# Grams moved beside the y products, state work moved one slot ahead, in a hybrid SSM and expert kernel

## The reference

```
lcs  = cumsum(dt * A)                       # decay sums inside the chunk
M    = exp(where(mask, lcs_l - lcs_i, -inf))
G    = C @ B^T                              # the gram of the chunk
y    = (M * G) @ x  +  exp(lcs) * C @ h     # own part + carried state
h    = exp(lcs_last) * h + (M_last * x)^T @ B
```

## Time and profile before

| | us |
|---|---|
| median of 3 runs | 580.51 (578.98 to 584.52) |
| profiled execution | 576.64 |
| its span, first to last instruction | 574.9 |
| PE busy in the span | 548.7 |
| DVE busy | 437.6 |
| ACT busy | 356.2 |
| POOL busy | 172.6 |

### The profile page before, as it was taken

The page is one execution under the profiler, slowest core; times in us unless marked ns, Lnnn a source line. Parts: engine busy times, 40 slices in busy tenths (PEclk is TensorE's granted clock), DMA queues, the critical chain, the costliest instruction groups (busy, mean ns, idle before and its releaser), DMA issues.

```text
span 574.9 us, 11864 instructions
## 1 busy us (share of the span) xinstructions
PE 548.7 (95%) x4016; PEld 429.8 (75%) x4016; DVE 437.6 (76%) x1037; ACT 356.2 (62%) x767; POOL 172.6 (30%) x232
## 2 busy tenths in 40 slices
PE   8886999999999999999999999999999999999996
PEld 7665767877777777877787777777778787777774
DVE  4878767887789785888688786987768787676654
ACT  3894488637675477636795477745787376852442
POOL 2073504521163202631046201622036210542011
PEclk9999999999999999999999999999999999999999
DMA  6650006300550006600272004700064003510120
GB/s 204 183 152 2 0 33 190 84 1 2 147 173 3 1 6 175 143 1 0 81 173 65 0 0 155 164 0 0 15 198 106 0 1 105 157 44 1 38 59 21
DMA packets 37354, 41.43 MB, mean 72 GB/s; under 512 B 3482, under 2 KB 27716, under 8 KB 37316
## 3 DMA queue, kind: packets, MB, share of 16 engines
q1 hardware_dynamic: 36724, 40.80, 25.9%
q10 hardware_dynamic: 592, 0.15, 0.1%
HBM read 37.79 MB, written 3.15 MB: 71 GB/s over the span
## 4 chain that ended last, share of the span: by engine, by line
PE 48%; DVE 19%; issue 11%; ACT 9%; DMA 5%; POOL 5%; SPq 1%; DVEq 0%; ACTq 0%; POOLq 0%
PE bank L424 7%; PE bank L426 5%; PE bank L425 5%; PE bank L535 4%; PE bank L642 4%; PE bank L644 4%; PE bank L643 4%; DVE act_l L1268 4%; DVE cv L1121 4%; DMA grow<-lc_rows 3%; ACT act_h L874 3%; PE bank L547 2%; PE bank L563 2%; PE bank L435 2%; ACT L967 2%
## 5 line engine op out<-in xcount | busy, mean ns | idle before, releaser
L1268 DVE SCALAR_TENSOR_TENSOR act_l<-bank,act_h 128x512 fp32r<-128x512 f32 x192 | 131.3, 686 | 69.8 <-ACT act_h L874 68.6
L874 ACT ACTIVATE act_h<-bank 128x512 fp32r<-128x512 f32 x192 | 114.1, 594 | 81.9 <-PE bank L426 78.0
L424 PE MATMUL bank<-fTl,w1h 128*128 128x512 f32 x192 | 86.9, 452 | 3.0 <-DVE fTl L1219 2.3
L1492 POOL TENSOR_TENSOR late<-late 128x512 f32<-128x512 f32 x31 | 39.8, 1285 | 163.3 <-DVE late L1276 163.3
L894 ACT ACTIVATE seg<-seg,lneg 128x128 f32<-128x128 f32 x256 | 81.2, 391 | 2.8 <-DMA seg<-lc_rows 2.8
L642 PE MATMUL bank<-act_l,w2h 128*128 128x512 f32 x192 | 77.5, 404 | 1.6 <-DVE act_l L1268 1.5
L425 PE MATMUL bank<-fTh,w1l 128*128 128x512 f32 x192 | 75.7, 394 | 0.0
L644 PE MATMUL bank<-act_h,w2h 128*128 128x512 f32 x192 | 75.6, 394 | 0.0
L426 PE MATMUL bank<-fTh,w1h 128*128 128x512 f32 x192 | 75.6, 394 | 0.0
L643 PE MATMUL bank<-act_h,w2l 128*128 128x512 f32 x192 | 75.2, 392 | 0.0
L1479 POOL TENSOR_TENSOR xw<-xs,seg 128x128 f32<-128x128 f32 x48 | 19.9, 414 | 157.3 <-ACT seg L894 82.8
(11 more groups left out here) (176 smaller groups left out, 1063.6 us busy)
## 6 DMA issues: line engine op xcount, KB each, us to landing
seg<-lc_rows SPq DMA_DIRECT2D x32, 512.0 KB, 4.5
late<-gk_rows SPq DMA_DIRECT2D x8, 1024.0 KB, 9.3
grow<-lc_rows SPq DMA_DIRECT2D x48, 128.0 KB, 5.4
x_in<-L_attn_hidden_dram SPq DMA_DIRECT2D x8, 256.0 KB, 3.7
out_dram<-late SPq DMA_DIRECT2D x8, 256.0 KB, 2.5
late<-L_ffn_sw_dram SPq DMA_DIRECT2D x2, 512.0 KB, 7.2
late<-L_ffn_rw_dram SPq DMA_DIRECT2D x1, 1024.0 KB, 7.7
CT<-L_attn_w_in_proj_dram SPq DMA_DIRECT2D x1, 512.0 KB, 5.3
```

The lines of the kernel that those rows point to most:

```text
L424: mm(dst, stat_h, mov_l, start=True, stop=False)
L874: nc.scalar.activation(act_h[:, b % RING, :], HID[b % 2][:], ACT.Relu).then_inc(act_h_ready, 1)
L1268: v_.scalar_tensor_tensor(act_l[:, r, :], HID[b % 2][:], 0.0, f(act_h[:, r, :]), ALU.max, ALU.subtract)\
```

## The change

1. Chunks 1 to 3 have their gram in front of the y product of the chunk before (inside `y_product`, step 2) and no longer in a step 1 of their own. Chunk 0's gram stays.
2. The chunk's own state product moves from step 2 to step 1 (`state_product`), and in sequences 1 to 7 DVE's state update moves with it (`next_state`, now in slots 13, 16 and 19, behind `act_l`).
3. DVE's `mg` of chunks 1 to 3 splits: the first half goes to slots 15, 18 and 21, the second to 16, 19 and 22, each **behind** the slot's `act_l`. In the opening it stays where it was.
4. `dta` and `kept` are stored with a stride of 32 columns per chunk, so that four 32-column matmuls become one of full width, in `lcs` and in `g_transposes`, where it becomes a transpose.
5. ACT copies B's fourth block ahead of the relu of slot 6, and moves `xs_copy(0)` from slot 5 to slot 6. DVE does only the first tap of the second convolution in slot 2, and the other three in slot 3.

```diff
 def lcs(s):
-    for c in range(NCH):
-        ins = mm(sums[32 * c:32 * c + 32, P:2 * P], dta[:, c * NH:c * NH + 32], upto[:], start=True, stop=True)
+    mm(sums[:, P:2 * P], dta[:].rearrange("p c q -> p (c q)"), upto[:], start=True, stop=True).then_inc(lcs_psum, 1)
...
+def state_product(s, c):
     if c > 0:
         pe.wait_ge(state_step, nth(s, 8, (2, 5, 8)[c - 1]))
+    pe.wait_ge(btok_ready, nth(s, 3, c + 1))
+    pe.wait_ge(xw_ready, nth(s, 6, 2 * c + 2))
+    for n in range(NP):
+        ins = mm(MAIN[1][:, n * 64:(n + 1) * 64], btok[:, at(n)], xw[:, n, :, :].rearrange("p t d -> p (t d)"),
+                 start=True, stop=True)
+    ins.then_inc(s_psum, 1)
+
+def y_product(s, c):
+    if c == NCH - 1:
+        pe.wait_ge(state_step, nth(s, 8, 8))
     if c < NCH - 1:
-        pe.wait_ge(btok_ready, nth(s, 3, c + 1))
-        pe.wait_ge(xw_ready, nth(s, 6, 2 * c + 2))
-        for n in range(NP):
-            ins = mm(MAIN[1][:, n * 64:(n + 1) * 64], btok[:, at(n)], xw[:, n, :, :].rearrange("p t d -> p (t d)"),
-                     start=True, stop=True)
-        ins.then_inc(s_psum, 1)
+        gram(s, c + 1, None)
...
-    if b == 0:
+    if b == 0 and c == NCH - 1:
         pe.wait_ge(mg_ready, nth(s, 8, 2 * c + 2))
...
 def g_transposes(s, prev):
-    for c in range(NCH):
-        ins = mm(MAIN[2][32 * c:32 * c + 32, 0:P], kept[:, c * NE:c * NE + 32], ident[:], start=True, stop=True)
-    ins.then_inc(gT_psum, 1)
+    nc.tensor.transpose(MAIN[2][:, 0:P], kept[:].rearrange("p c q -> p (c q)"), ident[:]).then_inc(gT_psum, 1)
...
 # PE, scan_part
-    if step == 1:
+    if step == 1 and c == 0:
         gram(s, c, prev)
+    if step == 1 and c < NCH - 1:
+        state_product(s, c)
...
 # ACT, body
+    if s is not None and i == 6:
+        b_copy(s, 3)
     if new := block_at(i, prev, older):
         relu(*new)
-    if s is not None and i in (5, 6):
-        b_copy(s, i - 3)
-        xs_copy(s, i - 5)
+    if s is not None and i == 5:
+        b_copy(s, 2)
+    if s is not None and i == 6:
+        xs_copy(s, 0)
+        xs_copy(s, 1)
...
 # DVE, body
     if (new := block_at(i, prev, older)) and not (i == 0 and prev is not None):
         act_low(*new)
+    if s is not None and i in (15, 18, 21):
+        masked_gram(s, i // 3 - 4, 0)
+    if s is not None and i in (16, 19, 22):
+        masked_gram(s, i // 3 - 4, 1)
+    if s is not None and i in (13, 16, 19):
+        next_state(s, i // 3 - 4)
...
-            conv(s, 1, (0, 1))
+            conv(s, 1, (0,))
         if i == 3:
-            conv(s, 1, (2, 3))
+            conv(s, 1, (1, 2, 3))
```

More of the change, by code:

```diff
@@ L180, in build @@
         rank = sb("rank", [P, NCH * NE])
-        kept = sb("kept", [P, (NCH - 1) * NE + 32])
+        kept = sb("kept", [P, NCH, 32])
         gT = sb("gT", [P, P])
@@ L704, in scan_part @@
                         b_tokens(s, c, prev, older)
-                    if step == 1:
+                    if step == 1 and c == 0:
                         gram(s, c, prev)
-                        if c == NCH - 1 and not is_seq(s, n_seq - 1):
-                            proj(s + 1, 0)
+                    if step == 1 and c < NCH - 1:
+                        state_product(s, c)
+                    if step == 1 and c == NCH - 1 and not is_seq(s, n_seq - 1):
+                        proj(s + 1, 0)
                     if step == 2:
@@ L785, in opening @@
                         b_tokens(0, c, None, None)
-                    gram(0, c, None)
+                    if c == 0:
+                        gram(0, c, None)
                     if c < 2:
@@ L1144, in c_copy @@
                 v_.tensor_copy(CT[:, b, :], MAIN[b][:]).then_inc(c_ready, 1)
-            def attend(s, c, step):
[L1147 to L1154, removed]
-                if step == 2:
[L1157 to L1173, removed]
@@ new lines, in masked_gram @@
+            def masked_gram(s, c, hf):
+                dve.wait_ge(g_psum, nth(s, 8, 2 * c + hf + 1))
+                dve.wait_ge(decay_masked, nth(s, 8, 2 * c + hf + 1))
+                if hf == 0 and (v := nth(s, 4, c)) is not None:
+                    dve.wait_ge(y_psum, v)
+                v_.tensor_tensor(mg[:, hf], MAIN[2 + hf][:].rearrange("p (n l) -> p n l", n=NP), decay(c)[:, hf], ALU.mult)\
+                    .then_inc(mg_ready, 1)
+            def attend(s, c, step):
+                if step == 1 and (c == 0 or is_seq(s, 0)):
+                    masked_gram(s, c, 0)
+                    masked_gram(s, c, 1)
+                if step == 2:
+                    if c < NCH - 1 and is_seq(s, 0):
+                        next_state(s, c)
@@ L1182, in attend, with next_state @@
                     v_.tensor_tensor(yT[:, :, at(c)], yT[:, :, at(c)], szT[:, :, at(c)], ALU.mult).then_inc(yz_ready, 1)
+            def next_state(s, c):
+                first = (0, 2, 5)[c]
+                if c > 0:
+                    dve.wait_ge(grow_ready, nth(s, 3, c))
+                    v_.tensor_tensor(state_m[:], state[:, (c - 1) % 2], grow[:, c % 2, :, P - 1:P].to_broadcast([P, NP, 2 * HD]),
+                                     ALU.mult).then_inc(state_step, 1)
+                    dve.wait_ge(state_step, nth(s, 8, first + 1))
+                    first += 1
+                dve.wait_ge(s_psum, nth(s, 3, c + 1))
+                own = MAIN[1][:, 0:256].rearrange("p (n d) -> p n d", n=NP)
+                for t in range(2):
+                    q, d = slice(64 * t, 64 * t + 64), slice(HD * t, HD * t + HD)
+                    if c == 0:
+                        v_.tensor_copy(state[q, c % 2, :, d], own[q, :, d]).then_inc(state_step, 1)
+                    else:
+                        v_.tensor_tensor(state[q, c % 2, :, d], own[q, :, d], state_m[q, :, d], ALU.add).then_inc(state_step, 1)
+                dve.wait_ge(state_step, nth(s, 8, first + 2))
             def mean_square(s):
@@ L1431, in opening @@
                                 channel_multiplier=1).then_inc(tables_set, 1)
-                for t, v in ((ones[:], 1.0), (upto[:], 1.0), (turn[:], 0.0), (lower[:], 1.0), (center[:], -1.0 / P), (dta[:, NCH * NH:], 0.0), (kept[:, NCH * NE:], 0.0)):
+                for t, v in ((ones[:], 1.0), (upto[:], 1.0), (turn[:], 0.0), (lower[:], 1.0), (center[:], -1.0 / P), (dta[:, :, NH:], 0.0), (kept[:, :, NE:], 0.0)):
                     g.memset(t, v).then_inc(zeros_set, 1)
```

12 lines of the change are left out of this document (6 added, 6 removed).

## The result

| | before | after |
|---|---|---|
| median, same chip, 4 runs each | 580.73 us | 607.31 us (606.22 to 613.5) |
| profiled execution | 576.64 us | 607.24 us |
| its span | 574.9 us | 605.5 us |
| mean distance from one `lcs` to the next, sequences 1 to 7 | 66.34 us | 70.38 us |

The ratio is **1.0497, interval 1.0448 to 1.0546**. On the median of 580.51 that is 609.4 us: slower, as forecast, but 8 us above the 601 predicted, and just beyond the range. It grew by 4.04 us, where +2.98 was forecast. Where a slot is said to grow, its length is taken from the first matmul of the first layer in the slot before to that in the slot itself.

The account below looks back on a forecast made before the run. TensorE, busy 548.7 of 574.9 us, was taken as the bound; 3.93 - 0.31 - 0.64 = +2.98 us for each of seven sequences, with opening and end +21.2, gave 601 us predicted, range 588 to 609.

Parts of the forecast that it names:

- the waits behind `act_l`: Slots 17, 20, 23: TensorE waits for the second `mg`, 2.42 us chain; 2 x 1.39 + 1.15 = 3.93 us per sequence lost.
- chunk blocks and state work: TensorE's gram, state and y product blocks: fewer tile-shape surcharges save 0.31 us per sequence, 0.61 as other bound.
- front part: Widened `lcs` and gate transpose, earlier copy of B: saves 0.64 us per sequence (0.2 to 1.3).
- the clock: Rival: each of 21 new waits drops TensorE's clock and loses some 1.6 us more; 635 us, chance 3%.
- Chunk 0 is spared: Chunk 0 adds no wait, as its `mg` stays ahead of `act_l`.
- worse: Rival: later `mg` of chunk 1 delays the decay reload two chunks on, up to 1 us more per sequence; 608, chance 6%.
- change of shape: Between state and y product on TensorE: its removal estimated at 0.07 us, three times per sequence (0.21).
- a full-width record: Widened TensorE matmuls: each full-width fp32 record costs about 0.116 us (0.93 / 8).
- The price of a gram in front of a y product: TensorE's joint blocks: kept at 1.09 us, the only price in the rows.

Follow-up runs that it names:

- e11: Kernel before with only the store's DMA moved behind the decay and growth reloads; 575.7 us against 578.09, ratio 0.9961.
- e7: e6 with the store's DMA moved behind the decay and growth reloads; 570.07 us, ratio 0.9884 against the kernel before.
- e8: Changed kernel with second `mg` ahead of `act_l`, store's DMA behind the reloads and `hn` moved from slot 18 to 19; 573.85 us, ratio 0.9936 against before.
- e5: Changed kernel with only the store's DMA moved behind the decay and growth reloads; 599.64 us against 577.56 for the kernel before, ratio 1.0400.
- e1: Changed kernel with DVE's second `mg` of chunks 1 to 3 ahead of `act_l` again; 586.7 us against 578.5 for the kernel before, ratio 1.0149.
- e2: Kernel before with only DVE's second `mg` of chunks 1 to 3 moved behind the slot's `act_l`; 597.6 us against 578.5, ratio 1.0323.
- e6: Kernel before with only the front part's edits (widened `lcs` and gate transpose, new ScalarE and convolution order); 580.23 us against 577.56, ratio 1.0024.
- e4: e1 with the state product and VectorE's state update back in step 2; 586.73 us, ratio 1.0136 against the kernel before.

## Why the prediction was right in kind and wrong in size

From before to after leads a path over four of the kernels (e11, e7, e8, e5), each read from one trace, so the period's +4.04 splits into their steps:

| step | from to | forecast | measured |
|---|---|---|---|
| the waits behind `act_l`, slots 17, 20, 23 | e8 to e5 | +3.93 | +3.64 |
| chunk blocks and state work | e7 to e8 | -0.31 | +0.04 |
| front part | e11 to e7 | -0.64 | -0.53 |
| store's chain, taken away from before | before to e11 | 0 | -0.29 |
| store's chain, put back into the change | e5 to after | 0 | +0.91 |
| the clock in sequence 1 | e5 to after | 0 | +0.27 |
| sum | before to after | +2.98 | +4.04 |

(`hn` leaves slot 18 from e7 to e8 and comes back from e8 to e5. With `mg` behind `act_l` it seems to make no wait of its own: slot 20 grows by 1.43 us (sequence 1 left out), and slot 17, with no `hn`, by 1.37. That is argued from the slots; no kernel had `hn` later and `mg` behind.)

**The added wait: right.** It is the largest term by far, its mechanism is in the rows (2.40 us where 2.42 was forecast), e1 takes it out of the changed kernel and e2 puts it into the kernel before. The slots, less what they grow in e8, give 1.37 + 1.43 + 1.04 = 3.84. What I missed is a refund: behind slot 23 TensorE is late, so the small wait for `act_l` in slot 0 ends by itself, -0.23.

**"Chunk 0 is spared": the step that failed.** True of the order of its `mg`, and I looked at nothing else. Chunk 0's `mg` also needs the decays, which hang on a reload, which stands behind a store in SyncE's queue, which waits for VectorE. That chain left 0.16 us of wait at the decays of sequence 4 before, and no room. What the front part brought TensorE to `lcs` sooner was paid back at the decays (e6), and the gram of chunk 1 in front of slot 14's y product made the rest. Net of what the chain cost before, that is 0.91 - 0.29 = 0.62 us of the period, and from `lcs` of sequence 2 to the end 7.7 us between e5 and the change, less 2.4 between e11 and before: some 5 us in all, the largest part of what was missing.

The sign stood in the trace of the kernel before. In its waits of TensorE, between the two lines shown in the earlier trace rows, there is a third:

```profile
PE bank L563 <- DVE mg L1153: 2.7, 5, 0.9
```

Three of these five are chunk 0's `mg`, in slot 14 of sequences 3, 6 and 7. One of them, 0.87 us long, is in the earlier trace rows, where I took from it only the 0.74 us from VectorE to TensorE, and did not ask why that `mg` was late.

Among the rivals, "worse" named late reloads, with up to 1 us per sequence, but of later chunks, through `mg` of chunk 1 freeing a buffer late. ScalarE's waits for DMAs tell the two apart. Before:

```profile
ACT grow L904 <- DMA grow<-lc_rows: 8.1, 10, 1.7
ACT seg L894 <- DMA seg<-lc_rows: 2.8, 6, 0.9
```

after:

```profile
ACT seg L900 <- DMA seg<-lc_rows: 7.4, 6, 1.7
ACT grow L910 <- DMA grow<-lc_rows: 3.0, 5, 1.0
```

The later chunks' reload (`grow`) costs ScalarE less than before; the wait that grew is that of chunk 0 (`seg`). e2 shows that the rival's path exists, but in the changed kernel it is not the one that decided. The path that did runs through a queue that I had not read: the prediction has no row of SyncE.

**The front part: right where it is, worth nothing in the whole.** Slots 4 to 10 save 0.55 in the changed kernel, and the period 0.53 from e11 to e7, for the 0.64 forecast. `act_l` of slot 7 caps it at slot 9, as foreseen (the wait of 0.45 at 297.48). But e6 shows that with the old store's place the kernel before gains nothing from it (1.0024).

**The blocks: the saving was booked, not earned.** Here are slot 22's matmuls in e8, where a gram stood before; what takes its place waits:

```profile
313.81 0.39 PE L645 MATMUL bank<-act_h,w2h 128*128 128x512 f32 x1
314.20 0.50 PE L424 MATMUL bank<-hTl,wh 128*128 128x512 f32 x1
```

The next sequence's projection starts 0.39 us after the matmul ahead of it instead of 0.23 (it seems to have caught up with `hTl`), and the next matmul 0.33 behind it instead of 0.23: 0.26 lost. In the changed kernel it is the same. Another 0.13 goes in slot 23 of e8, where the first `mg` matmul of the y product starts 0.37 us behind the carried state's instead of 0.24. The prices themselves came out near: in the rows of slot 16 above, a state product takes 0.81 us (313.08 to 313.89) up to a full-width matmul, and 0.93 in front of the 32-column tiles of the y product. So that change of shape costs 0.12 where I put 0.07, and a full-width record 0.10, not the 0.116 that I took from 0.93 / 8. By these prices the blocks should have saved 0.39 (+0.90 in slot 13, +0.26 in each of 14, 17 and 20, -0.39 in each of 16 and 19, -1.29 in slot 22), and the two places took it. The price of a gram in front of a y product I had right: 309.19 - 308.09 = 1.10 and 317.93 - 316.84 = 1.09, the 1.09 of a gram in front of a full-width matmul. A gram in front of 32-column tiles is no cheaper than one in front of a full-width matmul. The Trainium skill ("TensorEngine Tiling (Array Packing)", Tiling Modes) says that a change of mode drains TensorE. The trace agrees where it can be compared: 0.93 against 0.81 us for the same state product.

**The clock: a rival that happened once in the changed kernel's steady part.** Windows of TensorE in sequence 1 (stretch, us, busy, granted clock, DMA share, GB/s):

```profile
112.00:115.00 3.00, 1.16 (x20) 1.00 0.00 0
115.00:118.40 3.40, 3.40 (x39) 0.51 0.00 0
```

and what TensorE did there:

```profile
113.84 1.16 PE L533 MATMUL bank<-CT,BT 64*128 64x128 f32 x16 [1.98 <-DVE mg L1161]
```

One of the new waits was 1.98 us long, and the 3.4 us after it ran at 0.51, the 1.2 GHz level. From the last matmul of slot 19's first layer (110.77) to that of slot 20's it took 7.73 us, where sequences 3 to 6 took 5.5: 0.6 us of the 2.2 is the longer wait (1.98 instead of 1.38), and 1.6 the clock, as much as the rival named. The steady waits of 1.3 to 1.5 us left the clock where it was. In between, the length of a wait does not decide: behind 1.61 and 1.80 us in e2 and 1.90 in sequence 7 of e4 the clock fell, behind 1.77 us in sequence 1 of e5, the same place as here, it stayed at 1.00.

**The sum.** The span grew by 30.6 us where 21.2 were forecast. Of the 9.4, six times 1.06 (the period's excess, the clock's stretch in it) make 6.4. The other 3.0 lie at the two ends: up to `lcs` of sequence 1 the kernel grew by 0.45 us, and from `lcs` of sequence 7 to the end by 5.9 (101.5 against 95.6 us), together 6.3 where 3.3 was left of the forecast. Of the 5.9, 2.4 go when the store is moved (e5): in sequence 7 the decays wait longest, 1.7 us. The kernels with the new opening's grams differ among each other by up to 3 us up to `lcs` of sequence 1, with half-clock stretches at other places from trace to trace; what the opening costs on average stays open within that.

## What to carry to other kernels

In an in-order queue, an instruction's cost is set by what stands directly ahead of it: putting `mg` behind the one VectorE instruction that needs TensorE's freshest result tied TensorE to itself over three engines, 2.4 us a time. A saving upstream is worth only what the nearest chain beside it can follow: before booking it, follow each DMA that is reloaded in that stretch back through its queue, and ask whether an unrelated transfer stands ahead and what it waits for. Here moving one store behind the reloads was worth more (2.4 us in the kernel before; with the front part's edits 6 of the 10 us between e6 and e7) than every reordering of the matmuls.

## What the runs showed of the hardware

- A result's way across engines has a stable price, start to start, for 128x512: TensorE's last matmul to ScalarE 0.42 to 0.44 us, ScalarE to VectorE 0.63, one VectorE instruction to the next 0.61, VectorE to a waiting TensorE 0.74. The chain forecast from one kernel held in the other within 0.02.
- Idle stretches of 1.61, 1.80, 1.90 and 1.98 us in TensorE's steady part (e2 twice, e4, after) were each followed by some 3.4 us at half the clock, which cost 1.6 us where it could be measured. Others of 1.72 (e4) and 1.77 us (e5, e6) were not, nor were the recurring ones of 1.3 to 1.5, each between dense work.
- SyncE's DMA issues go in order, waits included: one store that stood ahead of a reload and waited for another engine held the reload back (1.86 us from the write of `lcsT` to the reload before, 2.69 after, 1.64 with the store behind). The reload also took longer to land behind the store: 4.0 to 4.8 us against 3.4 to 3.6.
- A state product of eight records takes 0.81 us up to a full-width matmul, 0.93 up to one in 32-column tiles. A gram in 64x128 tiles takes 1.09 to 1.10 up to either.
